# GpSimd's gathers of a block, issued in lots that wait for finished columns, in a two-layer graph kernel

## The chip, the cores and the metric

The kernel runs on one core of a Trainium2 chip. The metric is the device time in microseconds from the start to the end of one launch. Engines are named as in the profile: PE is TensorE (PEld its weight loads), DVE VectorE, ACT ScalarE, POOL GpSimd, SP SyncE.

## The reference

Two message-passing layers over 12,500 nodes with 16 features and 400,000 edges sorted by destination, each followed by a layer norm:

```
# layer 0: the 16x16 matrix of an edge comes from its 16 attributes
ew    = (edge_attr @ W_e + b_e).reshape(E, 16, 16)
msg   = einsum('ei,eio->eo', x[src], ew)
x     = layernorm(x + segment_sum(msg, dst) / max(count, 1) + bias)
# layer 1: the 16x16 matrix of an edge is one of 8, by its type; then a GRU cell
msg   = einsum('emh,eh->em', edge_emb[type].reshape(-1, 16, 16), x[src])
m     = segment_sum(msg, dst)
x     = layernorm(x + gru(m, x))
```

What costs is `x[src]`: 400,000 rows of 16 floats, looked up by index, in each layer.

## The kernel before

The edges are cut into 125 blocks of 3,200: 25 columns of 128 edges (one edge per partition). In both layers (`k` is 0 or 1) the same loop runs over the blocks, each engine with its own copy of it, two blocks per turn, and semaphores between them.

For each block the rows `x[src]` of the 25 columns come in two ways. **Gathered** columns are fetched by GpSimd with one indirect DMA each (L417): 16 columns in layer 0 and 15 in layer 1. **Picked** columns (`PICKED`, `H` = 9 in layer 0, 10 in layer 1) are made on chip: ScalarE builds one-hot matrices (`pick`, L468 and L474), TensorE multiplies them with the node table held in SBUF (`pick_rows`, L576: for each column four chunks, each against a high and a low part, so 8 matmuls with 8 weight loads, into one of 3 or 4 PSUM banks of `psN`), and VectorE masks and reduces the result (`select`, L723 and L727). The first block of a layer gathers all of its 25 columns.

The columns fall into three thirds (`START` = 0, 8, 16, 25). VectorE's `outer` (L752) forms, for a third j, the outer products `z` of the rows with the edges' coefficients. It waits for the third's gathers (`got`) and its picked columns (`sel`). TensorE's `sum_step` (L608) then adds the third into windows of 32 destinations with one-hot matrices: 8, 8 and 9 columns, each two matmuls and two weight loads.

TensorE's order in block b is: transposes of the sums before (L586, L587), the sum of third 0 of block b, pick 0 of block b+1, the result of the window before (L598, L599), picks 1 and 2, the sum of third 1, picks 3 to 5, the sum of third 2, picks 6 to 8 (to 9 in layer 1). So TensorE works on the picked columns of one block while it sums the block before.

VectorE's order in block b is: `outer` of third 1, the selects of picks 0 to 2 of block b+1, `outer` of third 2, four additions into the nodes (L709), the selects of picks 3 to 5, the matching of destinations (L736), `outer` of third 0 of block b+1, the remaining selects, and at the end the increment of `free` (L802), which says that the buffer of block b may be filled again.

GpSimd waits for `free` and for the indices (`idx`), and then issues the gathers of block b+2 into that buffer, third by third, with nothing in between. SyncE waits for each third's gathers before it loads the picks' sources for two blocks later (`src_mod`, L315).

The counts used in the waits: `picked` starts at 2H and rises by one when TensorE has finished a picked column; `sel` starts at H and rises by one for each column that VectorE has reduced; `z` starts at 3 and rises by one with each `outer`.

Of the kernel before, what the change touches and what calls it, by code (L numbers as in the profile page):

```python
# [16 lines left out]
NS = len(START) - 1  # L17
# [3 lines left out]
H = (9, 10)  # L21
# [4 lines left out]
GATHERED = [[[g for g in range(START[j], START[j + 1]) if g not in PICKED[:h]] for j in range(NS)] for h in H]  # L26
assert all(START[j] <= PICKED[t] < START[j + 1] for c in PCUT for j in range(NS) for t in range(c[j], c[j + 1]))
PAIRS = (((0, 1), (1, 3)), ((3, 4), (4, 6)), ((6, 7), (7, 9))), (((0, 2),), ((2, 4), (4, 6)), ((6, 8), (8, 10)))
SUB = 4
GPAD = -(-G // SUB) * SUB  # L30
WN = 32
# [7 lines left out]
ROW = 8  # L39
N_WIN, FIRST = SUB, SUB + 1  # L40
SUB_OF = [g % SUB for g in range(G)]
SUB_COLS = [SUB_OF.count(s) for s in range(SUB)]
COLUMN = [sum(SUB_COLS[:SUB_OF[g]]) + SUB_OF[:g].count(SUB_OF[g]) for g in range(G)]
FIRST_POS = [min(g for g in range(G) if SUB_OF[g] == s) for s in range(SUB)]
LAST_POS = [max(g for g in range(G) if SUB_OF[g] == s) for s in range(SUB)]


def build(nc, x, src, src_pick, dst, dst_rows_in, ea, etype, W_e, b_e, bias, A_t, w_ihT, w_hhT, b_ih, b_hh, out):
# [36 lines left out]
    with ExitStack() as ctx:  # L85
# [6 lines left out]
        def sem(name):  # L92
            return ctx.enter_context(nc.semaphore(name))
# [7 lines left out]
        z = [[m[:, 0:G * w].rearrange("p (g c) -> p g c", c=w) for m in z_mem] for w in (ZS, P)]  # L101
# [112 lines left out]
        s_turn = sem("s_turn")  # L214
        s_done = sem("s_done")
        L = []
        for k in range(2):
# [6 lines left out]
                picked=sem(f"l{k}_picked"), pick_act=sem(f"l{k}_pick_act"),  # L224
# [3 lines left out]
                z=sem(f"l{k}_z"), free=sem(f"l{k}_free"), coef=sem(f"l{k}_coef"), rel=sem(f"l{k}_rel"),  # L228
# [8 lines left out]
        def ln_cols(g):  # L237
            return slice(LN_AT[g], LN_AT[g + 1])

        def gate_cols(g0, g1):  # L240
            return slice(g0 * 2 * GB, g1 * 2 * GB)
# [164 lines left out]
        @block.gpsimd  # L406
        def _(pool):
            def gathers(k, table):
                l = L[k]

                def body(b, buf, r, whole=False):
                    pool.wait_ge(l["idx"][buf], 16 * (r + 1))
                    pool.wait_ge(l["free"], b + 1)
                    pool.sem_inc(s_turn)
                    for j in range(NS):
                        for g in range(START[j], START[j + 1]) if whole else GATHERED[k][j]:
                            pool.indirect_dma_start(  # L417
                                xs[k][buf][:, g, :], None, table,
                                bass.IndirectOffsetOnAxis(ap=idx[buf][:, g:g + 1], axis=0),
                            ).then_inc(l["got"][buf][j], 16)  # L420
                body(0, 0, 0, whole=True)
                with pool.Fori(0, (NB - 1) // 2) as i:
                    body(2 * i + 1, 1, i)
                    body(2 * i + 2, 0, i + 1)

            pool.iota(col_i[:], [[1, P]], base=0, channel_multiplier=0).then_inc(s_const, 1)
            pool.memset(ident[:], 0.0).then_inc(s_const, 1)
            pool.wait_ge(s_const, 2)
            pool.affine_select(out=ident[:], in_=ident[:], compare_op=ALU.not_equal, fill=1.0, base=0,
                               pattern=[[-1, P]], channel_multiplier=1).then_inc(s_const, 1)  # L430
            pool.iota(chunk_node_i[:], [[P, TC]], base=0, channel_multiplier=1).then_inc(s_const, 1)
            gathers(0, x)
            for g in range(N_LN - 1):
                cs = ln_cols(g)
                pool.wait_ge(s_nm, g + 1)
                pool.tensor_tensor(ya[:, cs, :], ya[:, cs, :], h[:, cs, :], ALU.add).then_inc(s_nh, 1)
            pool.wait_ge(s_hd, 16 * (N_LN + 1))
            gathers(1, h_dram)
            for g in range(n_gate):
                cs = gate_cols(g, g + 1)  # L440
                pool.wait_ge(s_n, g + 1)
                pool.tensor_tensor(yb[:, cs, :], h[:, cs, :], ya[:, cs, :], ALU.subtract).then_inc(s_pool, 1)
                pool.wait_ge(s_pool, g + 1)
                pool.tensor_tensor(yb[:, cs, :], yb[:, cs, :], rz[:, cs, F:2 * F], ALU.mult).then_inc(s_u, 1)
# [238 lines left out]
        def _(dve):  # L683
# [11 lines left out]
            def aggregate(k):  # L695
# [21 lines left out]
                def select(b, buf, t0, t1):  # L717

                    m, a, z_pos = t1 - t0, (H[k] * buf + t0) % RING[k], PICKED[t0:t1]
                    step_pos = z_pos[-1] - z_pos[0] if m == 2 else 1  # L720
                    dve.wait_ge(l["hot_g"], b + 1)
                    dve.wait_ge(l["picked"], H[k] * (b + 1) + t1)
                    dve.tensor_tensor(  # L723
                        cand[:, a:a + m], psN[:, a:a + m, 0:NG * F].rearrange("p m (f g) -> p m f g", g=NG),
                        grp_hot[:, t0:t1, :].unsqueeze(2).to_broadcast([P, m, F, NG]), ALU.mult).then_inc(l["cand"], m)
                    dve.wait_ge(l["cand"], H[k] * b + t1 + RING[k])
                    dve.tensor_reduce(xs[k][buf][:, z_pos[0]:z_pos[-1] + 1:step_pos, :], cand[:, a:a + m],  # L727
                                      AX.X, ALU.add).then_inc(l["sel"], m)
# [28 lines left out]
                def body(b, buf, r):  # L757
# [16 lines left out]
                    def selects(j):  # L774
                        for t0, t1 in PAIRS[k][j]:
                            select(*nxt[:2], t0, t1)
# [279 lines left out]
```

## Time and profile before

| | |
|---|---|
| time, median of 3 runs | 8332.13 us (8329.59 to 8337.34) |
| the profiled execution's own time | 8341.78 us |
| its span | 8340.0 us |
| mean granted clock of TensorE | 0.79 |
| PE busy, share of the span | 5873.7 us, 70% |
| DVE busy | 4257.7 us, 51% |
| POOL busy | 3698.0 us, 44% |
| ACT busy | 3415.6 us, 41% |

The profile is of one execution. A busy share is a mean over the whole span, so it hides that an engine may be idle in one part of every block and full in the other. "Issue", where it ends an idle stretch, means that the engine waited for nothing that the profile shows.

### The profile page before, as it was taken

Reading aid. Unit: us, or ns where it says so; the run is one execution under the profiler, and the core shown is the slowest. Engines: PE = TensorE matmul, PEld = TensorE weight load, DVE = VectorE, ACT = ScalarE, POOL = GpSimd, SP = SyncE. Lnnn points to the kernel's source line nnn. Section 1 sums busy time; section 2 is a strip of 40 time slices with the busy share of each in tenths; the row PEclk is TensorE's granted clock in tenths of the full one; section 3 lists DMA queues with packets and bytes.
Section 4 is the critical chain, followed back from the end, with each engine's and each line's share of the span. In section 5 each row is a group of like instructions: output and inputs, shape, how many; then the busy total and the mean of one; then the engine's idle time right before and its main releaser. Section 6 shows DMA issues by size and latency. Waiting matters only on the chain.

```text
span 8340.0 us, 118475 instructions
## 1 busy us (share of the span) xinstructions
PE 5873.7 (70%) x33300; PEld 4480.4 (54%) x33301; DVE 4257.7 (51%) x5509; ACT 3415.6 (41%) x6769; POOL 3698.0 (44%) x3920
## 2 busy tenths in 40 slices
PE   5777767777777777777766766776776776776776
PEld 4545545545555555455455555555555555555555
DVE  5555555555555555555544444444444444444444
ACT  4434434434444444344344443443443443443443
POOL 5444444444444444444344444444444444444443
PEclk8877878878878778778877777787777777777777
DMA  2111111111111111111111011011010001000001
GB/s 45 20 20 21 20 20 21 20 20 20 20 20 20 20 21 19 20 21 20 25 16 16 14 15 15 15 15 16 15 15 15 15 15 16 15 15 16 15 15 13
DMA packets 415049, 152.90 MB, mean 18 GB/s; under 512 B 240595, under 2 KB 414131, under 8 KB 414891
## 3 DMA queue, kind: packets, MB, share of 16 engines
q1 hardware_dynamic: 290248, 119.53, 6.9%
q0 software_dynamic: 124608, 32.15, 4.7%
q10 hardware_dynamic: 160, 0.80, 0.0%
q8 instruction: 18, 0.29, 0.0%
q14 instruction: 15, 0.12, 0.0%
HBM read 149.55 MB, written 2.56 MB: 18 GB/s over the span
## 4 chain that ended last, share of the span: by engine, by line
PE 54%; another core or an unknown queue 22%; issue 16%; DVE 7%; DVEq 1%; ACT 0%; DMA 0%; SPq 0%; ACTq 0%
PE psN L576 40%; PE psM L608 11%; DVE cand L723 3%; DVE z L752 2%; PE psR L598 1%; DVE nodeT L709 1%; PE psR L602 1%; PE psR L599 0%; DVEq L708 0%; PE psT L586 0%; PE psN L665 0%; PE psT L587 0%; PE psT L590 0%; DMA dst_mem<-in_dst_rows 0%
## 5 line engine op out<-in xcount | busy, mean ns | idle before, releaser
L576 PE MATMUL psN<-table_hi,pick 128*128 128x400 f32 x9424 | 3599.4, 382 | 230.4 <-issue 166.6
L576 PE MATMUL psN<-table_lo,pick 128*128 128x400 f32 x9424 | 3463.3, 367 | 228.4 <-issue 228.0
L723 DVE TENSOR_TENSOR cand<-psN,grp_hot 128x400 f32<-128x400 f32 (+1 forms) x1364 | 1190.7, 873 | 3772.1 <-remote 3410.1
L608 PE MATMUL psM<-z,onehot 128*32 128x273 f32 (+1 forms) x12500 | 1559.8, 397 | 1915.1 <-issue 1894.7
L417 POOL DMA_INDIRECT z<-in_x,idx x2009 | 1902.7, 947 | 2198.5 <-DVEq L802 1612.4
L417 POOL DMA_INDIRECT z<-h_rows,idx x1885 | 1781.3, 945 | 2346.3 <-DVEq L802 1792.7
L576 PEld LDWEIGHTS psN<-table_hi,pick 128*128 128x128 f32 x9424 | 1954.4, 207 | 589.9 <-issue 547.9
L576 PEld LDWEIGHTS psN<-table_lo,pick 128*128 128x128 f32 x9424 | 1952.7, 207 | 235.6 <-issue 232.5
L608 PEld LDWEIGHTS psM<-z,onehot 128*32 128x32 f32 x12500 | 554.6, 118 | 2831.7 <-issue 2767.9
L474 ACT ACTIVATE pick<-dist,one 128x384 fp32r<-128x384 f32 (+1 forms) x2976 | 1705.4, 621 | 125.7 <-remote 42.5
L485 ACT COPY sumS<-psM 128x273 f32<-128x273 f32 (+1 forms) x250 | 81.6, 326 | 3989.9 <-PE psM L608 3839.2
L468 ACT ACTIVATE dist<-src_mod,neg_node 128x384 f32<-128x384 uint16 (+1 forms) x2976 | 1708.2, 622 | 7.2 <-DMA src_mod<-src_mod_rows 7.2
L727 DVE TENSOR_REDUCE z<-cand 128x16 f32<-128x400 f32 (+1 forms) x1364 | 1190.2, 873 | 114.9
L752 DVE TENSOR_TENSOR z<-psD,z 128x1024 f32<-128x1024 f32 (+1 forms) x564 | 922.1, 1635 | 22.6 <-DMA z<-h_rows,idx 19.0
L752 DVE TENSOR_TENSOR z<-psN,z 128x2048 f32<-128x2048 f32 x186 | 441.2, 2372 | 0.0
L459 ACT COPY sumT<-psT 128x128 f32<-128x128 f32 x126 | 33.4, 265 | 541.5 <-PE psT L590 541.3
L736 DVE TENSOR_TENSOR onehot<-col_f,psR 128x800 f32<-128x800 f32 x250 | 245.9, 984 | 4.3
L709 DVE TENSOR_TENSOR nodeT<-nodeT,psR 17x32 f32 (+1 forms) x1008 | 178.9, 178 | 125.2 <-issue 52.6
L456 ACT COPY sumT<-psT 17x128 f32<-17x128 f32 x126 | 32.1, 255 | 181.4 <-PE psT L587 177.0
L714 DVE TENSOR_TENSOR grp_hot<-col_f,grp 128x225 f32<-128x225 f32 (+1 forms) x248 | 98.5, 397 | 0.2 <-DVE table_lo L809 0.2
L598 PE MATMUL psR<-sumT,W 128*17 128x128 f32 x504 | 77.5, 277 | 0.7 <-ACT sumT L457 0.7
L586 PE MATMUL psT<-ident,sumS 128*128 128x128 f32 x252 | 48.3, 273 | 38.5 <-issue 38.0
(106 smaller groups left out, 761.4 us busy)
## 6 DMA issues: line engine op xcount, KB each, us to landing
src_mod<-src_mod_rows SPq DMA_DIRECT2D x620, 96.0 KB
z<-in_x,idx POOLq DMA_INDIRECT x2009
z<-h_rows,idx POOLq DMA_INDIRECT x1885
eab<-in_edge_attr SPq DMA_DIRECT2D x125, 200.0 KB
src_mod<-src_mod_rows SPq DMA_DIRECT2D x124, 128.0 KB
idx<-in_src SPq DMA_DIRECT2D x250, 12.5 KB, 2.1
dstb<-in_dst SPq DMA_DIRECT2D x250, 14.0 KB, 1.6
grp<-src_grp SPq DMA_DIRECT2D x248, 5.0 KB
```

The lines of the kernel that those rows point to most:

```text
L417: pool.indirect_dma_start(xs[k][buf][:, g, :], None, table, bass.IndirectOffsetOnAxis(ap=idx[buf][:, g:g + 1], axis=0),).then_inc(l["got"] ...
L468: act.activation(dist[c % 2][:, 0:hi - lo], src_mod[buf][:, lo:hi], ACT.Abs, bias=neg_node[:, c:c + 1]).then_inc(l["dist"], 1)
L474: act.activation(pick[j][:, c, 0:hi - lo], dist[c % 2][:, 0:hi - lo], ACT.Relu, bias=one[:, 0:1], scale=-1.0).then_inc(l["pick_act"], 1)
L576: mm = pe.matmul(psN[:, bank(buf, t), 0:NG * F], pick[j][:, c, at:at + P], table_p[part][:, c * NG * F:(c + 1) * NG * F], start=(c == 0 an ...
L598: pe.matmul(psR[0:F + 1, 0:P], W0[:, c, :], sumT[:, c, :], start=(c == 0), stop=False)
L608: mm = pe.matmul(psM[s * WN:(s + 1) * WN, 0:W], onehot[buf][:, g, :], z[k][buf][:, g, 0:W], start=(g == FIRST_POS[s]), stop=(g == LAST_POS ...
L709: return dve.tensor_tensor(v, v, psR[p0:p1, s * WN:(s + 1) * WN], ALU.add).then_inc(l["acc"], 1)
L714: dve.tensor_tensor(grp_hot[:, 0:H[k], :], col_f[:, 0:NG].unsqueeze(1).to_broadcast([P, H[k], NG]), bc(grp[buf][:, 0:H[k]], NG), ALU.is_eq ...
L723: dve.tensor_tensor(cand[:, a:a + m], psN[:, a:a + m, 0:NG * F].rearrange("p m (f g) -> p m f g", g=NG), grp_hot[:, t0:t1, :].unsqueeze(2) ...
L727: dve.tensor_reduce(xs[k][buf][:, z_pos[0]:z_pos[-1] + 1:step_pos, :], cand[:, a:a + m], AX.X, ALU.add).then_inc(l["sel"], m)
L736: return dve.tensor_tensor(onehot[buf][:], col_f[:, 0:WN].unsqueeze(1).to_broadcast([P, G, WN]), bc(rel[buf][:, 0:G], WN), ALU.is_equal)
L752: dve.tensor_tensor(z[k][buf][:, cs, 0:n * F].rearrange("p g (k i) -> p g k i", i=F), coef[k][buf][:, cs, :].unsqueeze(3).to_broadcast([P, ...
```

## The change

Ahead of some gathers of a block, GpSimd now waits for work on that same block's other columns. `n` counts the gathers of the block from 0. `AFTER_PICK` gives the picked column that TensorE must have finished (by its number t), `AFTER_SEL` how many columns VectorE must have reduced, and `AFTER_OUTER` the third whose `outer` must be done. In layer 0 the gathers so go in the lots 0-1, 2, 3, 4-6, 7, 8, 9-10, 11-12, 13-14, 15; in layer 1 in 0-1, 2, 3, 4-6, 7, 8, 9, 10-11, 12, 13-14. After each such wait there is one increment of `s_turn`, which nothing waits for. The first block of a layer, which gathers all 25 columns, has none of these waits. The gathers themselves, their order and their number stay.

```diff
--- before.py
+++ after.py
@@ -26,6 +26,11 @@
 GATHERED = [[[g for g in range(START[j], START[j + 1]) if g not in PICKED[:h]] for j in range(NS)] for h in H]
 assert all(START[j] <= PICKED[t] < START[j + 1] for c in PCUT for j in range(NS) for t in range(c[j], c[j + 1]))
 PAIRS = (((0, 1), (1, 3)), ((3, 4), (4, 6)), ((6, 7), (7, 9))), (((0, 2),), ((2, 4), (4, 6)), ((6, 8), (8, 10)))
+AFTER_PICK = ({0: 2, 2: 3, 3: 4, 4: 5, 7: 6, 8: 7, 9: 8}, {0: 2, 2: 3, 3: 4, 4: 5, 7: 6, 8: 7, 9: 8, 10: 9})
+AFTER_SEL = ({13: 9}, {12: 8, 13: 10})
+AFTER_OUTER = ({11: 0, 15: 1}, {})
+assert all(t < H[k] for k in range(2) for t in AFTER_PICK[k].values())
+assert all(AFTER_OUTER[k][n] < j for k in range(2) for n in AFTER_OUTER[k] for j in range(NS) if sum(len(GATHERED[k][i]) for i in range(j)) <= n < sum(len(GATHERED[k][i]) for i in range(j + 1)))
 SUB = 4
 GPAD = -(-G // SUB) * SUB
 WN = 32
@@ -412,8 +417,19 @@
                     pool.wait_ge(l["idx"][buf], 16 * (r + 1))
                     pool.wait_ge(l["free"], b + 1)
                     pool.sem_inc(s_turn)
+                    n = 0
                     for j in range(NS):
                         for g in range(START[j], START[j + 1]) if whole else GATHERED[k][j]:
+                            if not whole:
+                                if n in AFTER_PICK[k]:
+                                    pool.wait_ge(l["picked"], H[k] * (b + 1) + AFTER_PICK[k][n] + 1)
+                                if n in AFTER_SEL[k]:
+                                    pool.wait_ge(l["sel"], H[k] * b + AFTER_SEL[k][n])
+                                if n in AFTER_OUTER[k]:
+                                    pool.wait_ge(l["z"], NS * (b + 1) + AFTER_OUTER[k][n] + 1)
+                                if n in AFTER_PICK[k] or n in AFTER_SEL[k] or n in AFTER_OUTER[k]:
+                                    pool.sem_inc(s_turn)
+                            n += 1
                             pool.indirect_dma_start(
                                 xs[k][buf][:, g, :], None, table,
                                 bass.IndirectOffsetOnAxis(ap=idx[buf][:, g:g + 1], axis=0),
```

On GpSimd's own queue, a block of layer 0 stands like this before the change (`idx`, `free`: the waits at a block's start; the row with x15 stands for the other gathers of the block):

```order
L422 ISA
L413 ISA [waits l0_idx1]
L417 DMA z<-in_x,idx 128x16 [waits l0_free]
L417 DMA z<-in_x,idx 128x16 x15
L412 ISA
L413 REGISTER_ALU [waits l0_idx0]
```

After the change the first seven gathers of the same block, up to the waits for picks 6 and 7, stand like this (an ISA or REGISTER_ALU row holds the wait's count; the wait itself stands at the gather behind it):

```order
L418 ISA [waits l0_idx1]
L425 ISA [waits l0_free]
L433 DMA z<-in_x,idx 128x16 [waits l0_picked]
L433 DMA z<-in_x,idx 128x16
L425 REGISTER_ALU
L433 DMA z<-in_x,idx 128x16 [waits l0_picked]
L425 REGISTER_ALU
L433 DMA z<-in_x,idx 128x16 [waits l0_picked]
L425 REGISTER_ALU
L433 DMA z<-in_x,idx 128x16 [waits l0_picked]
L433 DMA z<-in_x,idx 128x16 x2
L425 REGISTER_ALU
```

One run of gathers has become five lots here, each behind a wait for `picked`. The rest of the block, from gather 11 on, with the start of the next block behind it:

```order
L433 DMA z<-in_x,idx 128x16 [waits l0_picked]
L425 REGISTER_ALU
L433 DMA z<-in_x,idx 128x16 [waits l0_picked]
L433 DMA z<-in_x,idx 128x16
L429 ISA
L433 DMA z<-in_x,idx 128x16 [waits l0_z]
L433 DMA z<-in_x,idx 128x16
L427 ISA
L433 DMA z<-in_x,idx 128x16 [waits l0_sel]
L433 DMA z<-in_x,idx 128x16
L429 REGISTER_ALU
L433 DMA z<-in_x,idx 128x16 [waits l0_z]
```

These last lots wait for VectorE (`z` and `sel`), and the next block's first gather now waits for `picked` too, behind the wait for `free`.

## Rows read from the trace of the kernel before

**Rows 1.** Page, part 1, busy time
```profile
PE 5873.7 (70%) x33300; PEld 4480.4 (54%) x33301; DVE 4257.7 (51%) x5509; ACT 3415.6 (41%) x6769; POOL 3698.0 (44%) x3920
```

**Rows 2.** Waits: engine, line <- releaser: us, times, longest us
```profile
DVE cand L723 <- remote: 3410.1, 254, 31.9
...
PEld psM L608 <- issue: 2767.9, 2813, 3.4
PE psM L608 <- issue: 1894.7, 1787, 3.2
```

**Rows 3.** GpSimd's timeline: start, us, engine line op xcount, idle before
```profile
2016.38 0.94 POOL L417 DMA_INDIRECT z<-in_x,idx  x1 [12.93 <-DVEq L802]
...
2035.11 0.95 POOL L417 DMA_INDIRECT z<-in_x,idx  x1 [0.30 <-issue]
2049.16 0.94 POOL L417 DMA_INDIRECT z<-in_x,idx  x1 [13.11 <-DVEq L802]
```

**Rows 4.** Windows of one block, layer 0, columns as headed
```profile
core 0: us, PE busy (x) PEld busy (x) DVE busy (x) ACT busy (x) POOL busy (x), PEclk, DMA share, GB/s
2016.38:2024.16 7.78, 7.78 (x54) 6.37 (x54) 6.76 (x6) 6.62 (x13) 5.95 (x7) 1.00 0.07 5
2024.16:2025.70 1.54, 1.54 (x9) 1.26 (x7) 1.26 (x4) 0.00 (x0) 1.24 (x2) 1.00 0.23 37
2025.70:2038.89 13.19, 3.81 (x8) 1.12 (x8) 0.34 (x2) 0.00 (x0) 7.92 (x9) 0.66 0.11 19
2038.89:2048.96 10.07, 10.06 (x61) 7.88 (x61) 9.42 (x12) 6.34 (x15) 0.00 (x0) 0.77 0.14 32
```

**Rows 5.** TensorE's timeline in the same block
```profile
2020.15 0.34 PE L576 MATMUL psN<-table_lo,pick 128*128 128x400 f32 x1
...
2024.87 0.34 PE L576 MATMUL psN<-table_hi,pick 128*128 128x400 f32 x1
2025.05 0.34 PE L576 MATMUL psN<-table_lo,pick 128*128 128x400 f32 x1
...
2034.69 0.61 PE L608 MATMUL psM<-z,onehot 128*32 128x273 f32 x1 [1.49 <-issue]
...
2038.89 0.73 PE L608 MATMUL psM<-z,onehot 128*32 128x273 f32 x4 [0.79 <-issue]
```

**Rows 6.** GpSimd's timeline, early in layer 0
```profile
32.63 2.55 POOL L417 DMA_INDIRECT z<-in_x,idx  x1 [0.30 <-issue]
35.48 0.94 POOL L417 DMA_INDIRECT z<-in_x,idx  x1 [0.30 <-issue]
...
60.49 0.94 POOL L417 DMA_INDIRECT z<-in_x,idx  x1 [0.30 <-issue]
```

**Rows 7.** TensorE's timeline behind those gathers
```profile
63.53 0.61 PE L608 MATMUL psM<-z,onehot 128*32 128x273 f32 x1 [1.49 <-issue]
64.93 1.98 PE L608 MATMUL psM<-z,onehot 128*32 128x273 f32 x10 [0.78 <-issue]
```

**Rows 8.** GpSimd's timeline, one block of layer 1
```profile
6013.43 0.94 POOL L417 DMA_INDIRECT z<-h_rows,idx  x1 [13.82 <-DVEq L802]
...
6030.90 0.94 POOL L417 DMA_INDIRECT z<-h_rows,idx  x1 [0.31 <-issue]
6046.61 0.94 POOL L417 DMA_INDIRECT z<-h_rows,idx  x1 [14.77 <-DVEq L802]
```

**Rows 9.** Windows of that block, layer 1, columns as in rows 4
```profile
6013.43:6021.93 8.50, 8.49 (x58) 7.53 (x57) 5.17 (x9) 6.98 (x13) 6.60 (x7) 1.00 0.07 6
6021.93:6035.40 13.47, 3.90 (x18) 1.51 (x18) 0.70 (x1) 0.01 (x1) 7.54 (x8) 0.68 0.14 26
```

**Rows 10.** TensorE's timeline in that block
```profile
6033.15 0.37 PE L608 MATMUL psM<-z,onehot 128*32 128x128 f32 x1 [0.97 <-issue]
6034.56 0.80 PE L608 MATMUL psM<-z,onehot 128*32 128x128 f32 x9 [1.04 <-issue]
```

**Rows 11.** GpSimd's timeline, block with a late second gather
```profile
2641.89 0.94 POOL L417 DMA_INDIRECT z<-in_x,idx  x1 [1.74 <-issue]
```

## The prediction

> **What bounds the kernel now.** The page's busy shares come first [rows 1]: TensorE is busy for 70% of the span and no engine for more, so nothing is full on average. The table of waits says where the rest goes [rows 2]: VectorE waits 3410 us at its selects (L723) for something that the profile calls remote, and TensorE itself sits idle at L608, 2768 us at the weight loads and 1895 us at the matmuls, with "issue" as the reason: it waits for no semaphore. So the bound is a TensorE that could go on and doesn't, and the question is when.
>
> The windows of one block of layer 0 answer that [rows 4]. It starts with the block's first gather, at 2016.38 [rows 3]. For 9.3 us TensorE runs at full rate: 54 + 9 matmuls and 54 + 7 weight loads, 124 in all. Then, from 2025.70 to 2038.89, 13.19 us, it issues 8 and 8. Then come 61 and 61 in 10.07 us. In the slow stretch a matmul takes 0.61 us and has 1.49 us of idle time before it [rows 5]. VectorE is busy for 0.34 us of it and ScalarE for none: they wait for TensorE. GpSimd alone is busy. This happens once a block; a block takes 2049.16 - 2016.38 = 32.8 us [rows 3].
>
> When does it end? Not with the last gather (2035.11, done at 2036.05) but 2.8 us later. From the first gather to TensorE's return it is 2038.89 - 2016.38 = 22.51 us for 16 gathers [rows 3, 5], 1.407 us each. In layer 1 it is 6034.56 - 6013.43 = 21.13 us for 15 [rows 8, 10], 1.409 each. Early in layer 0, 21 gathers stand without a break from 35.48 to 60.49, and TensorE is back at 64.93 [rows 6, 7]: 29.45 / 21 = 1.402. Three counts, one price. But GpSimd issues them (2035.11 - 2016.38) / 15 = 1.249 us apart. My reading: each gather loads something that TensorE's instructions need too for 1.41 us, GpSimd adds one each 1.25 us, the debt grows, and TensorE lives on a reserve of about 124 instructions until the debt is gone. What that something is no row says.
>
> The third count carries more. Gathers had gone on before 35.48 too, yet the count works only from there. Just before, one took 2.55 us and not 0.94 [rows 6]. So a pause of some 1.6 us wipes the debt. That is what the change could use.
>
> **The change part by part.** It removes nothing. It adds 10 waits to each block of both layers, 124 blocks each (the first block of a layer has none), and as many increments.
>
> *The added instructions.* They stand on GpSimd, which is idle 12.93 us between two blocks' gathers [rows 3], so I cost them at nothing by themselves. Queued behind each wait are the rest of the block's gathers, and behind those the next block's; VectorE's `outer` and SyncE's source loads wait for them.
>
> *Where the waits bind.* I count from the end of pick 2, where gather 0 may now go. In the profiled block that is 2020.15 + 0.34 = 2020.49, so the gathers start 4.1 us later than now [rows 3, 5]. At full rate matmuls of a pick stand 0.18 us apart [rows 5], so a pick takes 8 x 0.18 = 1.45 us. Gathers 0, 1, 2, 3 and 4 thus go about as fast as picks 3, 4 and 5 get done, 5 and 6 follow, and 7 waits for pick 6. TensorE has by then issued 32 + 48 + 36 = 116 instructions (sum 1, picks 3 to 5, sum 2), so its reserve ends inside pick 6. GpSimd stops at gather 7, the debt of 7 gathers is paid after 7 x 1.41 = 9.8 us, TensorE gets its full rate back, pick 6 ends and gather 7 goes. Gathers 7 to 15 find their conditions met soon after: 9 x 1.41 = 12.7 us. The next pause is the next block's gather 0, which waits for pick 2.
>
> *The stall that is left.* One stretch of 22.5 us with 9.3 us free in it becomes two, and TensorE gets the free part twice: (9.8 - 9.3) + (12.7 - 9.3) = 3.9 us of stall against 22.5 - 9.3 = 13.2 now. Saved: 9.3 us a block in layer 0. In layer 1 the free part is 8.5 us [rows 9], and by the same rule that is what is saved there.
>
> *What the pauses cost.* A gather behind a fresh release starts later than one in a run, where 0.30 us lie between two [rows 3]. The one late gather that I found had 1.74 us before it [rows 11]. So a restart costs 0 to 1.4 us, and two of them a block bind. Most of that lies beside TensorE's free part; I take 0.7 us a block, nearer the ordinary row. On the other side, the clock falls to 0.66 of full speed on average in the slow stretch and is 0.77 in the 10.07 us after it [rows 4], which would be 7.8 us at full clock. Shorter stalls may give back 0 to 2.3 us. I leave this at nothing, and let it stand in the range against the restarts.
>
> *The sum.* Layer 0: 124 x (9.3 - 0.7) = 1066 us. Layer 1: 124 x (8.5 - 0.7) = 967 us. Against the profiled execution's own 8341.8 us: 8341.8 - 2033 = 6309. The median of the runs lies 9.7 us lower, so **6300 us**.
>
> *Floors.* 31 gathers at 1.407 us are 43.6 us for a block of each layer, against 32.8 + 33.2 = 66.0 now [rows 3, 8]. If that pace became the only bound, 124 x (66.0 - 43.6) = 2780 us would be saved: about 5560 us. VectorE has 6.76 + 1.26 + 0.34 + 9.42 = 17.8 us of work in a block of layer 0 [rows 4], which is under 22.5.
>
> **A rule against it.** By the rows, gathers issued later cost nothing as long as GpSimd has 12.93 us to spare. The Trainium skill (DMA: Bandwidth & Descriptors, Rules for kernel authors) says the opposite of this change: issue a DMA early, compute, and wait late. By that rule the 4.1 us are a pure loss, the slower case below. It also says (SBUF - State Buffer, SBUF: two separate sides) that a DMA and a compute engine cannot slow each other, by which the waits would change nothing for TensorE. The trace does not agree with the second: TensorE's slow stretch follows the number of gathers three times over.
>
> **The rivals.**
>
> *The waits close a ring (slower).* If a pause does not pay the debt, TensorE starves inside a pick whose end GpSimd waits for. 16 instructions then take 16 x 0.82 = 13 us (13.19 us for 16 [rows 4]). Even if only the start moves, by 4.1 us, and each block grows by that: 8332 + 248 x 4.1 = 9350 us. It decides once TensorE stays slow for more than about 2 us after GpSimd stopped at a wait. For it: one engine waits for the other both ways. Against it: [rows 6, 7] count afresh after a pause.
>
> *The runs of gathers hardly break.* If the stop at gather 7 is too short, and say gathers 4 to 15 stay one run, the stall is 12 x 1.41 - 9.3 = 7.6 us, and 5.6 are saved: 8332 - 248 x (5.6 - 0.7) = 7117 us. For it: a pick's 1.45 us against a gather's 1.41 leaves almost no gap at gathers 2 to 4, and VectorE's conditions for 11, 13 and 15 are met early.
>
> *Nothing happens.* TensorE's slowness has another cause that only falls together with the gathers, and the later start lies in idle time: 8332 us. The three counts speak against it.
>
> **How the numbers follow.** Two free stretches a block (5600 to 6900 us): 0.65. Runs that hardly break (6900 to 7600): 0.16. Less gain than that: 0.04. No change: 0.03. Slower: 0.12. The range holds the first two cases, 5600 to 7600, down to the floor of the gathers' pace. A change within 0.2%, 17 us, could not be told from none: faster 0.85, same 0.03, slower 0.12.
>
> **What the profile after would show.** If right: gathers in two or more groups a block, the first after pick 2, with a gap before gather 7 or near it; TensorE's "issue" idle at L608 and L576 down by two thirds; in windows of one block slow stretches of under 4 us, each ending about 1.41 us times the gathers since the last gap; a block of 24 to 25 us; a mean clock above 0.79. VectorE's 3410 us of waiting for a remote releaser should fall to under half. The prediction is wrong if slow stretches of over 10 us remain after a pause, or if GpSimd never pauses inside a block, or if VectorE's `outer` (L752) starts to wait for late gathers.

## The result, and the profile after

The changed kernel takes 6356.2 us (median of 4 runs, 6347.98 to 6360.66), the kernel before 8334.7 us in the same comparison (8329.59 to 8351.9). The ratio is 0.762, with a 95% interval of 0.761 to 0.764. On two other chips, met later, the kernel before takes 4975 us and the change costs 0.9%; that has its own place among the experiments.

The page of the changed kernel, part 1, and then its table of waits (engine, line, releaser: us, times, longest). Its lines stand 16 further down than before: L592 is the picks' line, L624 the sums', L739 the select's, L768 `outer`, L433 the gathers'.

```profile
PE 5313.6 (84%) x33300; PEld 4306.0 (68%) x33301; DVE 4267.7 (67%) x5509; ACT 3422.3 (54%) x6769; POOL 3700.0 (58%) x3920
```

```profile
DVE cand L739 <- remote: 1266.4, 239, 6.0
...
PEld psM L624 <- issue: 1125.7, 1602, 5.7
...
POOL z L433 <- PE psN L592: 756.5, 445, 7.5
PE psM L624 <- issue: 692.4, 746, 5.4
```

Against [rows 1, 2] no engine has less work, but TensorE's "issue" idle time at the sums fell from 4663 to 1818 us and VectorE's remote wait from 3410 to 1266. The table puts 445 of GpSimd's waits down to TensorE. Its timeline shows the lots of one block of layer 0, gathers 7 to 15, and of the next, gathers 0 to 7:

```profile
2006.62 0.94 POOL L433 DMA_INDIRECT z<-in_x,idx  x1 [1.67 <-PE psN L592]
...
2016.60 0.95 POOL L433 DMA_INDIRECT z<-in_x,idx  x1 [0.30 <-issue]
2020.51 0.94 POOL L433 DMA_INDIRECT z<-in_x,idx  x1 [2.96 <-remote]
2021.77 0.94 POOL L433 DMA_INDIRECT z<-in_x,idx  x1 [0.31 <-issue]
2025.23 0.94 POOL L433 DMA_INDIRECT z<-in_x,idx  x1 [2.52 <-PE psN L592]
2027.03 0.94 POOL L433 DMA_INDIRECT z<-in_x,idx  x1 [0.85 <-PE psN L592]
2028.48 0.94 POOL L433 DMA_INDIRECT z<-in_x,idx  x1 [0.50 <-issue]
...
2032.22 0.94 POOL L433 DMA_INDIRECT z<-in_x,idx  x1 [0.30 <-issue]
```

There are two long pauses, ahead of gathers 0 and 2, and gathers 2, 3 and 4 go 1.8 and 1.45 us apart, not 1.25. Which of these pauses the new waits make is seen beside the last matmuls of the picks that they wait for. Pick 6 (for gather 7), pick 2 (for gather 0) and pick 3 (for gather 2):

```profile
2003.50 0.34 PE L592 MATMUL psN<-table_lo,pick 128*128 128x400 f32 x1
...
2015.13 0.34 PE L592 MATMUL psN<-table_lo,pick 128*128 128x400 f32 x1 [1.53 <-issue]
...
2023.89 0.54 PE L592 MATMUL psN<-table_lo,pick 128*128 128x400 f32 x1
```

Gather 2 starts 0.80 us after its pick's end, and so (0.81 and 0.82) do gathers 4 and 3: these waits bind. Gather 0 starts 5.04 us after the end of pick 2, and gather 7 2.78 us after the end of pick 6; GpSimd had ended the gather ahead of them at 2017.55 and 2004.94, and by then their waits were met: VectorE had passed the increment of `free` before 2011.61, and the indices were issued at 1993.28. Still GpSimd stood for 2.96 and 1.67 us, the first time until 1.15 us after TensorE's return at 2019.36. So these two pauses are not made by the waits that stand ahead of them, though the timeline names a pick for one. From 5012 to 5037 us, in layer 1, the same three waits bind and the same two don't. The windows of the same 25.6 us, cut where TensorE's pace changes:

```profile
core 0: us, PE busy (x) PEld busy (x) DVE busy (x) ACT busy (x) POOL busy (x), PEclk, DMA share, GB/s
2006.62:2013.60 6.98, 6.98 (x49) 5.08 (x47) 4.82 (x6) 6.70 (x15) 5.46 (x6) 1.00 0.08 14
2013.60:2019.36 5.76, 1.15 (x3) 0.53 (x4) 0.30 (x1) 0.00 (x0) 3.03 (x4) 0.90 0.11 13
2019.36:2025.23 5.87, 5.87 (x26) 4.66 (x26) 5.58 (x6) 3.15 (x6) 1.89 (x2) 0.52 0.28 60
2025.23:2032.22 6.99, 6.99 (x49) 5.86 (x48) 5.95 (x10) 3.02 (x7) 4.72 (x5) 1.00 0.06 6
```

The slow stretch is 5.76 us long, against 13.19 [rows 4]; counted from TensorE's first to the end of its last "issue" idle of over 0.3 us, it is the longest of the eleven in layer 0 between 2000 and 2280 us, which last 3.1 to 5.8 us, 4.7 on average. It ends 2019.36 - 2006.62 = 12.74 us after the first of 9 gathers in a row: 1.416 us each. During the gathers 2 to 6 there is none. Behind the slow stretch the clock is 0.52, near the lower of its two levels. The same in a block of layer 1, from its gather 7 on:

```profile
5024.46:5031.35 6.89, 6.88 (x49) 5.54 (x47) 4.83 (x6) 6.89 (x14) 5.36 (x6) 1.00 0.10 14
5031.35:5035.77 4.42, 0.81 (x3) 0.32 (x4) 0.00 (x0) 0.57 (x2) 2.17 (x3) 0.98 0.11 15
5035.77:5048.38 12.61, 12.61 (x83) 11.75 (x84) 10.82 (x16) 6.90 (x15) 6.61 (x7) 0.87 0.14 25
```

8 gathers, 11.31 us until TensorE is back: 1.414 each. Two windows of 2000 us, one in each layer, give the mean block, since the fifth group counts the gathers:

```profile
1000.00:3000.00 2000.00, 1692.45 (x10055) 1279.41 (x10053) 1384.68 (x1692) 1040.23 (x2147) 1159.94 (x1230) 0.90 0.15 26
4000.00:6000.00 2000.00, 1695.33 (x11123) 1469.50 (x11122) 1308.15 (x1757) 1142.14 (x2173) 1184.21 (x1256) 0.93 0.14 21
```

2000 x 16 / 1230 = 26.0 us in layer 0 and 2000 x 15 / 1256 = 23.9 in layer 1, against the 32.8 and 33.2 of the two blocks in [rows 3, 8]; the same two windows of the kernel before give 32.8 and 33.1. 124 x (6.8 + 9.3) = 1996 us; the two profiled executions are 8341.8 - 6356.1 = 1986 apart.

### The profile page after: what moved, and what is told of

Read it like the earlier page. It is cut to its first block, busy times and chain, and to the rows that moved or that the text cites. A ratio compares the mean times of both kernels' runs of the same rounds, so it can differ in the third digit from the quotient of the medians.

```text
span 6354.2 us, 123249 instructions
## 1 busy us (share of the span) xinstructions
PE 5313.6 (84%) x33300; PEld 4306.0 (68%) x33301; DVE 4267.7 (67%) x5509; ACT 3422.3 (54%) x6769; POOL 3700.0 (58%) x3920
## 4 chain that ended last, share of the span: by engine, by line
PE 74%; issue 16%; another core or an unknown queue 4%; DVE 3%; ACT 1%; DMA 1%; POOL 1%; DVEq 1%; ACTq 0%; POOLq 0%; SPq 0%
PE psN L592 55%; PE psM L624 15%; DVE cand L739 1%; DVE z L768 1%; DMA z<-in_x,idx 1%; PE psR L614 1%; PE psR L618 1%; POOL z L433 1%; ACT dist L484 1%; PE psR L615 0%; ACT pick L490 0%; DVEq L780 0%; PE psT L602 0%; PE psN L681 0%
## 5 line engine op out<-in xcount | busy, mean ns | idle before, releaser
L592 PE MATMUL psN<-table_hi,pick 128*128 128x400 f32 x9424 | 3533.9, 375 | 117.8 <-issue 83.6
L592 PE MATMUL psN<-table_lo,pick 128*128 128x400 f32 x9424 | 3394.1, 360 | 99.5 <-issue 98.9
L433 POOL DMA_INDIRECT z<-in_x,idx x2009 | 1905.4, 948 | 1354.8 <-issue 556.3
L433 POOL DMA_INDIRECT z<-h_rows,idx x1885 | 1780.7, 945 | 1231.8 <-issue 605.0
L592 PEld LDWEIGHTS psN<-table_hi,pick 128*128 128x128 f32 x9424 | 1902.9, 202 | 466.7 <-issue 277.7
L739 DVE TENSOR_TENSOR cand<-psN,grp_hot 128x400 f32<-128x400 f32 (+1 forms) x1364 | 1190.1, 872 | 1426.2 <-remote 1266.4
L592 PEld LDWEIGHTS psN<-table_lo,pick 128*128 128x128 f32 x9424 | 1900.5, 202 | 118.4 <-issue 116.4
L624 PE MATMUL psM<-z,onehot 128*32 128x273 f32 (+1 forms) x12500 | 1129.1, 381 | 714.3 <-issue 692.4
L624 PEld LDWEIGHTS psM<-z,onehot 128*32 128x32 f32 x12500 | 487.9, 118 | 1241.0 <-issue 1125.7
L768 DVE TENSOR_TENSOR z<-psD,z 128x1024 f32<-128x1024 f32 (+1 forms) x564 | 922.6, 1636 | 279.1 <-DMA z<-h_rows,idx 162.7
L768 DVE TENSOR_TENSOR z<-psN,z 128x2048 f32<-128x2048 f32 x186 | 441.9, 2376 | 96.2 <-DMA z<-in_x,idx 95.5
L614 PEld LDWEIGHTS psR<-sumT,W 128*17 128x17 f32 x504 | 39.2, 97 | 52.8 <-issue 49.5
L602 PEld LDWEIGHTS psT<-ident,sumS 128*128 128x128 f32 x252 | 34.7, 140 | 45.7 <-issue 37.2
```

The costliest lines, as they stand in the source:

```text
L433: pool.indirect_dma_start(xs[k][buf][:, g, :], None, table, bass.IndirectOffsetOnAxis(ap=idx[buf][:, g:g + 1], axis=0),).then_inc(l["got"] ...
L592: mm = pe.matmul(psN[:, bank(buf, t), 0:NG * F], pick[j][:, c, at:at + P], table_p[part][:, c * NG * F:(c + 1) * NG * F], start=(c == 0 an ...
L614: pe.matmul(psR[0:F + 1, 0:P], W0[:, c, :], sumT[:, c, :], start=(c == 0), stop=False)
L624: mm = pe.matmul(psM[s * WN:(s + 1) * WN, 0:W], onehot[buf][:, g, :], z[k][buf][:, g, 0:W], start=(g == FIRST_POS[s]), stop=(g == LAST_POS ...
L739: dve.tensor_tensor(cand[:, a:a + m], psN[:, a:a + m, 0:NG * F].rearrange("p m (f g) -> p m f g", g=NG), grp_hot[:, t0:t1, :].unsqueeze(2) ...
L768: dve.tensor_tensor(z[k][buf][:, cs, 0:n * F].rearrange("p g (k i) -> p g k i", i=F), coef[k][buf][:, cs, :].unsqueeze(3).to_broadcast([P, ...
```

## Experiments

The theory (debt), as the prediction has it: each gather costs the engines' instruction supply 1.41 us, so a debt grows while gathers go 1.25 us apart, and a pause pays it. The rivals: a fixed stall for each block; GpSimd's own work as the cause; the late start alone as what helps. Chips are given by number, and each kernel is compared with the kernel before on its own chip. Each experiment is one run but for r1_after.

### Chip 2: parts of the change (before: 8388.6 us)

**e1_start**: only the first of the ten waits.

```diff
-AFTER_PICK = ({0: 2, 2: 3, 3: 4, 4: 5, 7: 6, 8: 7, 9: 8}, {0: 2, 2: 3, 3: 4, 4: 5, 7: 6, 8: 7, 9: 8, 10: 9})
-AFTER_SEL = ({13: 9}, {12: 8, 13: 10})
-AFTER_OUTER = ({11: 0, 15: 1}, {})
+AFTER_PICK = ({0: 2}, {0: 2})
+AFTER_SEL = ({}, {})
+AFTER_OUTER = ({}, {})
```

> Of the ten waits a block only the first is left: gather 0 waits for pick 2, and the rest follow in one run. Debt theory (each gather loads something that TensorE needs for 1.41 us, a pause clears it): the run of 16 is as long as before, so TensorE is slow until 22.5 us after the first gather in layer 0 (21.1 in layer 1), about 13 us a block; the start only moves by 4.1 us, beside the part of TensorE's work that it overlaps. Time 8100 to 8700 us. Placement rival (the gain comes from where the gathers lie against TensorE's picks, not from the breaks): most of the gain is kept, 6400 to 7000 us. Ring rival (a later start is a pure loss of 4.1 us a block): 9350 us.

Measured: 8251.5 us. GpSimd's timeline, and TensorE's last delayed matmul behind the second of these gathers:

```profile
2003.54 0.94 POOL L433 DMA_INDIRECT z<-in_x,idx  x1 [13.45 <-PE psN L592]
...
2038.09 0.94 POOL L433 DMA_INDIRECT z<-in_x,idx  x1 [14.89 <-PE psN L592]
```

```profile
2060.83 0.49 PE L592 MATMUL psN<-table_hi,pick 128*128 128x400 f32 x1 [0.91 <-issue]
```

2060.83 - 2038.09 = 22.7 us for 16 gathers without a break: the price per gather is the old one, and the late start is worth 1.6% by itself, in one run. It neither brings the 24% (the rival wanted 6400 to 7000 us) nor costs its 4.1 us a block.

**e2_two**: the waits ahead of gathers 0 and 7, which are the two that the prediction counts on.

```diff
+AFTER_PICK = ({0: 2, 7: 6}, {0: 2, 7: 6})
+AFTER_SEL = ({}, {})
+AFTER_OUTER = ({}, {})
```

> Two waits a block are left: gather 0 for pick 2 and gather 7 for pick 6, so two runs of 7 and 9 gathers (7 and 8 in layer 1). Debt theory, as the prediction walked it: these are the two that bind, so the time is near that of the change, 6200 to 6700 us, with slow stretches of TensorE that end 1.41 us times the gathers since the last pause. Rival (it takes all ten waits, each small gap counts): over 7000 us.

Measured: 6644.9 us, 0.792 of before, against the whole change's 0.762. So two waits bring most of it and the other eight the rest: 3.0% of 8335, 250 us; which of the eight was not tried. GpSimd's timeline of a block, and the matmuls at which TensorE's pace returns:

```profile
2007.04 0.94 POOL L433 DMA_INDIRECT z<-in_x,idx  x1 [5.63 <-PE psN L592]
...
2014.53 0.94 POOL L433 DMA_INDIRECT z<-in_x,idx  x1 [0.30 <-issue]
2018.97 0.94 POOL L433 DMA_INDIRECT z<-in_x,idx  x1 [3.50 <-PE psN L592]
...
2028.96 0.94 POOL L433 DMA_INDIRECT z<-in_x,idx  x1 [0.30 <-issue]
2034.06 0.94 POOL L433 DMA_INDIRECT z<-in_x,idx  x1 [4.15 <-PE psN L592]
```

```profile
2016.97 0.45 PE L592 MATMUL psN<-table_lo,pick 128*128 128x400 f32 x1 [0.36 <-issue]
...
2031.77 0.35 PE L592 MATMUL psN<-table_lo,pick 128*128 128x400 f32 x1 [1.75 <-issue]
```

Here both waits bind: gather 7 starts at 2018.97, 0.81 us after pick 6's end, and gather 0 at 2034.06, 0.82 us after pick 2's. The first run has 7 gathers, and TensorE is back 9.93 us after its first: 1.42 each. The second has 9, and it is back after 12.80: 1.42 each. A fixed stall for each block is out: the delay follows the gathers since the last pause.

### Chip 2: the gathers' spacing, and GpSimd without gathers

**e4_space16**: no wait of the change; GpSimd clears a spare tile of 128 x 16 ahead of each gather. (In this diff, as in the runs below with other widths, `pace` is the spare tile and `s_pace` orders its two halves.)

```diff
+        pace = [sb(f"pace{i}", [P, 16]) for i in range(2)]
...
+                            if not whole:
+                                pool.wait_ge(s_pace[k], (25 - H[k]) * (b - 1) + n + 4)
+                                pool.sem_inc(s_turn)
+                                pool.memset(pace[n % 2][:], 0.0).then_inc(s_pace[k], 1)
+                                n += 1
                             pool.indirect_dma_start(
```

> The kernel before without any wait of the change; between gathers GpSimd writes zeros to a spare tile of 16 columns, which makes the gathers' distance longer. Debt theory: if the distance comes out above 1.41 us, no debt ever grows and TensorE has no slow stretch at all; the block is then bound by GpSimd, 16 and 15 times the distance (at 1.6 us: 25.6 and 24.0 us, 6400 us in all). If it stays under 1.41 us the slow stretch begins later and ends at the same count. Placement or wait rival (what helps is that gathers follow TensorE's progress): the slow stretch of 13 us stays and the longer run of gathers adds to it, 8300 to 9500 us.

Measured: 8497.4 us. GpSimd's timeline shows why this does not test what it was made for:

```profile
2001.10 0.95 POOL L425 DMA_INDIRECT z<-in_x,idx  x1 [0.57 <-POOL pace L423]
2002.05 0.12 POOL L423 MEMSET pace<- 128x16 f32 x1
2002.35 0.95 POOL L425 DMA_INDIRECT z<-in_x,idx  x1 [0.18 <-POOL pace L423]
```

The 0.12 us fit into the 0.30 that lie between two gathers anyway, and the distance stayed 1.25 us. It does show that work of GpSimd's between the gathers pays no debt. TensorE's first and last delayed matmuls behind the gather at 2001.10, the first of its block:

```profile
2009.41 0.45 PE L585 MATMUL psN<-table_hi,pick 128*128 128x400 f32 x1 [1.26 <-issue]
...
2023.77 0.49 PE L585 MATMUL psN<-table_hi,pick 128*128 128x400 f32 x1 [1.62 <-issue]
```

It is back 22.67 us after the first of 16 gathers, 1.42 each. Why the run is 1.3% slower stays open; it is one run.

**e6_nodma**: each gather of a block is replaced by two writes on GpSimd, of a constant into its 16 columns and of zeros into 768 spare ones (0.85 us together). No row is fetched for these columns, so the output is not the reference's.

```diff
-                            pool.indirect_dma_start(
-                                xs[k][buf][:, g, :], None, table,
-                                bass.IndirectOffsetOnAxis(ap=idx[buf][:, g:g + 1], axis=0),
-                            ).then_inc(l["got"][buf][j], 16)
+                            pool.memset(xs[k][buf][:, g, :], 0.5).then_inc(l["got"][buf][j], 16)
```

> The kernel before with every gather left out and replaced by a GpSimd write of a constant to the same column, with a write of 768 columns to a spare tile ahead of it to keep GpSimd as busy; the looked-up rows are constants here, so the output is not the reference's. Debt theory (the load is of the gathers' transfers): TensorE has no slow stretch, a block takes TensorE's and VectorE's own work, 19 to 20 us, about 5000 us in all, or GpSimd's own 16 times its op if that is longer. Rival (any work of GpSimd slows TensorE): slow stretches stay, with GpSimd's busy time as their length.

Measured: 4732.9 us, with a mean clock of 0.993. Page, part 1:

```profile
PE 4608.7 (97%) x33300; PEld 3912.2 (83%) x33301; DVE 4246.7 (90%) x5509; ACT 3417.2 (72%) x6769; POOL 3072.6 (65%) x7764
```

TensorE is full. GpSimd's own work is not the cause; the gathers are, and without them this chip runs the rest in 56% of the time. SyncE's loads are all still there, so they don't cause it by themselves either.

### Chips 6 and 5: where the price is not charged

**e8_space128, e9_space272, e7_space384** and **e5_direct** were to find the distance at which no debt grows, and whether a DMA without indices costs the same. The first three differ from e4_space16 in the width of the spare tile only.

> As the run with 16 spare columns, with 128: the gathers' distance should come to about 1.34 us (0.95 for the gather, 0.18 behind the write, 0.21 for the write), still under 1.41. Debt theory: the debt never reaches zero inside a block, the slow stretch of TensorE stays and ends 22.5 us (21.1) after the first gather; time 8300 to 8600 us. Rival (any slack between gathers helps in proportion): the slow stretch is half as long, under 7700 us.

> 272 spare columns: distance about 1.46 us, a little over 1.41, and no wait of the change. Debt theory in its sharp form: the debt is zero ahead of each gather, no slow stretch, and the block is GpSimd's 16 x 1.46 = 23.4 us and 15 x 1.46 = 21.9 plus the restart of about 0.7: near 5900 us, faster than the change. In a soft form (the reserve fills slowly in a pause of 0.05 us): slow stretches are left, 6500 to 8000 us. If the price per gather is no such threshold, the time is that of the run with 128 columns.

> 384 spare columns: distance about 1.55 us, well over 1.41. Debt theory: no slow stretch, block 16 x 1.55 = 24.8 and 15 x 1.55 = 23.3 us plus 0.7, near 6300 us. Rival (TensorE's slow stretch belongs to the gathers being under way, whatever their distance, or gathers must follow TensorE's progress): 8400 us or more.

e5_direct fetches 128 rows in order, and not by index, so its rows are the wrong ones:

```diff
+                                pool.dma_start(xs[k][buf][:, g, :], table[g * P:(g + 1) * P, :]).then_inc(l["got"][buf][j], 16)
```

> The kernel before, with each gather of the blocks behind the first replaced by a plain transfer of the same 128 rows of 64 bytes from GpSimd's queue, without indices; the rows are the wrong ones, so the output is not the reference's. If the load on TensorE is of the transfer's descriptors or packets, the slow stretch stays about as long per transfer as before, and shows a distance of its own. If it is of the index lookup in GpSimd's gather, there is no slow stretch, and the time is near that of the run without transfers, 4700 to 5500 us.

They ran on chip 6, and there the kernel before takes **4975.3 us**, not 8389. So none of the four tests what it was sent for. Measured: 5382.4, 5828.8, 6194.9 and 4741.1 us. What they do show is the bound on such a chip. e9_space272's distance, in GpSimd's timeline:

```profile
2002.29 0.95 POOL L425 DMA_INDIRECT z<-in_x,idx  x1 [0.17 <-POOL pace L423]
2003.23 0.35 POOL L423 MEMSET pace<- 128x272 f32 x1
2003.75 0.95 POOL L425 DMA_INDIRECT z<-in_x,idx  x1 [0.17 <-POOL pace L423]
```

1.46 us against 1.25: 0.21 more for each of the 124 x 31 = 3844 gathers is 807 us, and 5828.8 - 4975.3 = 854. GpSimd's gathers set the pace there. With plain DMAs in their place TensorE does (e5_direct: busy for 4607.3 of 4739.3 us).

**r1_after** is the changed kernel on chip 5, timed against the kernel before.

> The changed kernel once more, beside the kernel before, because the last four runs found the kernel before at 4975 us and not at 8330 to 8390: there the gathers did not slow TensorE. If this chip is one where the kernel before takes about 8350 us, the change takes about 6350 us again. If it is one where the kernel before takes about 4975 us, there is no debt for the waits to pay, they only delay gathers: gather 0 starts 4 us later in a block of 19 to 20 us, of which GpSimd needs 20.0 us for 16 gathers without a pause, so GpSimd becomes the bound and the change is slower, 5100 to 5500 us. Rival: the change makes no difference there, 4975 us.

Measured: 5020.7 us (2 runs, 5020.60 to 5020.76) against 4976.6 (3 runs, 4974.32 to 4979.44): ratio 1.009, interval 1.006 to 1.012: slower by 0.9%, little but more than the noise. One block in the windows, then the DMA queue of the gathers on the page of r1_after and, in the last fence, on that of the changed kernel in the main comparison:

```profile
1506.03:1526.21 20.18, 19.21 (x135) 15.39 (x134) 18.31 (x24) 13.93 (x30) 15.10 (x17) 1.00 0.23 33
```

```profile
q0 software_dynamic: 124608, 32.15, 8.0%
```

```profile
q0 software_dynamic: 124608, 32.15, 6.1%
```

GpSimd issues gathers all the time (15.10 us busy at 0.94 each, 1.25 apart), and TensorE issues 135 matmuls and 134 weight loads beside them at full clock, with no slow stretch. The gathers' packets take 8.0% of 5018.8 us here, 401, and 6.1% of 6354.2 there, 388. So neither the gathers' issue nor, to within 3%, the time of their packets differs. What they do to the engines does. The change's waits nearly always find their condition met, but GpSimd is the bound here, and what little it loses costs time: 44 us.

**r2_space272** and **r3_space272** repeat e9_space272 on chip 5.

> The gathers 1.46 us apart (a write of 272 spare columns between them, no wait of the change) once more. Where the kernel before takes 4975 us it was bound by GpSimd, 5829 us, and should be again. Where the kernel before takes about 8350 us: debt theory, sharp form, no slow stretch and again about 5850 us, under the change; soft form (a pause of 0.05 us behind each gather clears little), 6500 to 8000 us; rival (the slow stretch belongs to gathers under way, whatever their distance), 8400 us or more.

> The kernel of before (no waits of the change), with GpSimd clearing a spare tile of 128 x 272 between the gathers, so that one gather goes each 1.46 us and not each 1.25; it took 5829 and 5831 us on two chips on which the kernel of before takes 4975. What it tells hangs on the chip: where the kernel of before takes 8300 to 8400 us, the debt theory (each gather costs TensorE's instructions 1.41 us of supply, so that at 1.46 us apart no debt builds up) expects no stretch of slow issue and 5750 to 6000 us. A softer form of it (supply lags at any distance near 1.4 us, because TensorE also needs supply of its own) expects 6300 to 7600 us. The rival that a block's 15 gathers together cost a fixed time expects 8300 to 8600 us. Where the kernel of before takes about 4975 us again, all expect 5830 us.

Measured: 5831.2 and 5830.4 us, again beside a kernel before of 4977.

**r4_before** is the kernel before, run for its trace; it came to chip 12.

> The kernel of before, unchanged, for a trace of its own. Where it takes 8300 to 8400 us, its trace should be that of the rows read before the prediction: a stretch of some 13 us of TensorE instructions at one per 0.8 us in each block. Where it takes about 4975 us, the theory that the gathers slow TensorE's supply on some chips only expects the same distance of gathers (1.25 us, 0.94 us each on GpSimd) with no such stretch, an issue idle time of TensorE at the sums under a tenth of the 4662 us of before, and a granted clock near full. The rival that the gathers themselves run otherwise there (shorter, or further apart) expects another distance or another duration of them.

Measured: 8348.1 us, and 8351.5 for the run beside it: the slow kind again, with the page of [rows 1] nearly number for number:

```profile
PE 5918.8 (71%) x33300; PEld 4496.3 (54%) x33301; DVE 4258.7 (51%) x5509; ACT 3416.1 (41%) x6769; POOL 3707.2 (44%) x3920
```

So the kernel before has two times: 8330 to 8390 us in the main comparison and on chips 2 and 12, 4974 to 4979 on chips 5 and 6. No kernel was seen at both on one chip.

## Why the prediction was right, step by step

- **The total** (6300, measured 6356): right in sign and within 1%. That it came so near is luck, for two misses cancel. Predicted savings were 8.6 us a block in layer 0 and 7.8 in layer 1; measured 6.8 and 9.3.
- **The price of a gather, 1.41 us, counted from the last pause**: right, and shown by e1_start (16 in 22.7 us), e4_space16 (16 in 22.67), e2_two (7 in 9.93, 9 in 12.80) and the changed kernel (9 in 12.74, 8 in 11.31).
- **"So a pause of some 1.6 us wipes the debt"** [rows 6]: came true, but was read from too little. Two more gathers just before had taken 3.40 us (at 25.24) and 2.12 (at 30.20). It is the changed kernel that shows it: behind a pause of 1.67 us the count starts afresh.
- **The stall that is left** ("(9.8 - 9.3) + (12.7 - 9.3) = 3.9 us"): mis-sized. It is 5.76 us in layer 0's block and 4.42 in layer 1's, all in the second run. The 12.7 was right, the free 9.3 was not: TensorE goes on for 6.98 us and 49 + 47 instructions, not 124. It is tempting to say that a short pause (1.67 us ahead of gather 7) pays the debt but fills the reserve only in part. The runs don't bear that out. In e4_space16 TensorE goes on for 7.05 us (from 2001.10 to 2008.15) behind 14.35 us in which GpSimd was idle, and in the changed kernel the free part behind pauses of 1.65 to 1.93 us lasts from 5.7 to 9.6 us. So a fixed reserve of 124 instructions is wrong, and what sets the free part stays open.
- **Where the waits bind** ("gathers 0 to 4 go about as fast as picks 3, 4 and 5 get done"; only 0 and 7 were counted): the step that was wrong in kind. In the changed kernel the waits ahead of 2, 3 and 4 bind, 2.52, 0.85 and 0.50 us of idle time, and those ahead of 0 and 7 do not: GpSimd does stop there, but for no wait that the trace shows, and ahead of gather 0 until 1.15 us after TensorE is back. It looks held as TensorE is. So the break in front of gather 7 came, and for another reason than the predicted one. Where the two waits do bind (e2_two), they bring 0.792; with the other eight it is 0.762, 250 us more. No stall falls on gathers 2 to 6. That their slower pace, 1.8 and 1.45 us against the price of 1.41, is the reason is argued and not shown: five gathers at 1.41 owe 7.05 us, and TensorE goes on for 5.7 us or more anyway, so little stall could fall on them at any pace. That the waits for VectorE (11, 13, 15) are met early was right: behind gather 7 no gap shows in the block.
- **The clock** (left at nothing): right for layer 0's block, by balance. The 5.87 us at 0.52 hold 26 matmuls; 0.33 us from one pick matmul to the next there against 0.18 at full clock [rows 5]. Before, 10.07 us ran at 0.77 [rows 4]. In layer 1 it did give something back. Before, behind the slow stretch of [rows 9]:

```profile
6035.40:6046.61 11.21, 10.78 (x59) 9.90 (x59) 9.86 (x14) 6.61 (x14) 0.00 (x1) 0.77 0.06 8
```

That is 11.21 us at 0.77, and in the changed kernel 12.61 us at 0.87: some 2.6 and 1.6 us lost to the clock, an estimate from these two rows, so about 1 us a block given back. It is part of why layer 1 saved more than forecast.

- **The restarts** (0.7 us a block): not separated. A gather behind a wait that binds starts 0.80 to 0.82 us after the end of the pick. In the single blocks shown, the stretch is 13.19 - 5.76 = 7.4 us and 13.47 - 4.42 = 9.1 us shorter [rows 4, 9], about what the blocks got shorter (6.8 and 9.3). Counted over more blocks (eight of before and eleven after in layer 0, six and ten in layer 1, from 2000, 6000 and 5000 us on), it is 7.7 us shorter in layer 0 and 7.6 in layer 1. So in layer 0 some 0.9 us a block goes elsewhere, and the restarts may be in it.
- **The views named ahead**: VectorE's wait under half (37%) and the clock above 0.79 (0.911) came. The block of 24 to 25 us (26.0 and 23.9) and the "issue" idle down by two thirds (61% at the sums, 59% with the picks) came nearly; slow stretches of under 4 us did not (5.76, 4.42). And one of the three signs of being wrong came: `outer` did begin to wait for late gathers, 371 us in all by the table of waits, against 19 before. It was not enough to undo the rest, so as a sign it was badly chosen.
- **The ring** did not close, and a stop of 1.67 us was enough to keep the next debt apart. **The rule to issue early and wait late** (the Trainium skill, DMA: Bandwidth & Descriptors, Rules for kernel authors) lost where gathers cost TensorE time and held, by 0.9%, where they don't. By **the rule of the two sides** (the Trainium skill, SBUF - State Buffer, SBUF: two separate sides) a DMA does not slow a compute engine: r1_after, with TensorE at full clock beside the gathers, agrees with it; 8388.6 us with the gathers against 4732.9 without them, on chip 2, does not. Whether SBUF has a part in that no run shows.
- **"VectorE and ScalarE wait for TensorE"** was a misreading, for VectorE at least. In the changed kernel the last matmul of pick 0, and then VectorE's select of it:

```profile
2009.46 0.35 PE L592 MATMUL psN<-table_lo,pick 128*128 128x400 f32 x1
```

```profile
2019.47 0.57 DVE L739 TENSOR_TENSOR cand<-psN,grp_hot 128x400 f32<-128x400 f32 x1 [5.56 <-remote]
```

The pick was ready by 2009.81, and the group mask that the select also needs by 2009.59. VectorE was idle for the last 5.56 us ahead of 2019.47 and began 0.11 us after TensorE was back. So VectorE is held as TensorE is, and "remote" is here no wait for another engine's work. GpSimd's stop ahead of gather 0 has the same name and, by the rows above, the same look; 618 us in 220 stops of GpSimd's are put down to it. On chip 5 no such wait is among the rows of VectorE's table.

**What stays open.** What a gather loads for 1.41 us, what sets TensorE's free part, and why all this only on some chips or occasions. GpSimd's own work is excluded (e6_nodma), as are longer transfers or another pace of issue (r1_after). Whether DMAs without indices charge it, and whether a distance of 1.46 us avoids it, was tried only where no price is charged. If it does, e9_space272 would take some 5830 us on the slow kind too and beat the change; that is a guess from the debt's arithmetic, not a result.

## What to carry to other kernels

If an engine idles on "issue" in stretches that start some us after a run of indirect DMAs and end at a fixed price times their number, count the price from the last pause. If it is above the distance at which they are issued, break the run with a wait for work on the other engines. Two breaks a block brought 21% here, and ten waits 24%; whether an even pace at the price itself does as well was not tried on a chip that charges it. Read the place of a break from the trace, by the time between the end of the work waited for and the start behind it, and not from the name of the releaser. Time the kernel before on several chips first. Here the same change is worth 24% on one kind and costs 0.9% on the other.

## What the hardware showed that was not expected

- Two times for one kernel, 8335 and 4975 us, by chip or occasion. The changed kernel's traces of both kinds (6354 and 5019 us) have the same gathers and packets.
- On the slow kind, 16 gathers, whose data are 128 rows of 64 B each, hold TensorE and VectorE for 13.2 us in each 32.8.
- VectorE's instructions are held with TensorE's, and the profile names the wait "remote". GpSimd itself stops too, its next gather starting 1.15 us after TensorE's return.
